# Columns of tiles 16 to 31 from a second layout of x, and a first block whose carry, counts and store come one to two steps later

## The chip, the cores and the metric

The kernel runs on one core of a Trainium2 chip. What is timed is the device time of one execution in microseconds (us). Three executions of the kernel before took 832.69, 831.65 and 831.66 us; the median is 831.66 us.

## The reference: what is computed

x is 4096 rows of 512. A first part normalizes each row (layer norm, then an RMS norm), projects it with a 512 x 512 matrix, and adds a row of a context table, chosen by running sums over a mask. That table is a linear recurrence over 3202 context rows. A second part is a layer norm and a feed-forward network of hidden size 2048. Cut to what matters:

```python
x = x + xattn(_layernorm(x), ctx_2048, mask, W_in, b_in, g_res, g_init)
#   h = rmsnorm(embeds, g_res) @ W_in.T + b_in
#   s[t] = a * s[t-1] + dt * bcoef * (rmsnorm(ctx, g_init)[t, :512] / dt)
#   plug = clip(cumsum(boundary_mask) - 1, 0, plen - 1)
#   xattn = s[plug] + h
x = x + gelu(_layernorm(x) @ w1 + b1) @ w2 + b2
```

## The kernel before, in words

**Two stages.** The first stage takes x in 32 tiles of 128 rows (steps t = 0 to 31 of a Python loop that is written out on every engine). The second takes 8 groups of 512 rows through the two feed-forward products. All products are in split precision: a float32 operand is written as a high part plus a low part, and three matmuls (high by high, low by high, high by low) stand for one. L889 to L891 are these three.

**One tile of the first stage.** TensorE needs the tile with its columns on the partitions. In the kernel before, tiles 0 to 19 are loaded in rows and transposed by TensorE (`transpose_first`, L872, four 128x128 transposes into a PSUM bank). Tiles 20 to 31 (`HOSTED`) come a second time, from an array `x_cols` in which x is already laid out by columns; SyncE loads them into free quarters of `w_raw` (L445), and `columns(t)` (L195) says where they are. ScalarE rounds the columns to the high part (`tile_high`, L717), VectorE subtracts to get the low part (`tile_low`, L1070), TensorE makes the twelve 512-wide matmuls of `project(t)` (L893), and VectorE scales the result and adds x (`tile_add`, L1078). Each engine keeps its own order: at step t VectorE first does `tile_add(t-1)`, then `tile_low(t+2)`, then whatever else the loop puts at that step, then the statistics of a later tile (L1065, L1066). `project(t)` waits for `tile_low(t)` and, through its PSUM bank, for `tile_add(t-3)`.

**The context blocks beside the tiles.** The recurrence runs over blocks of 512 rows, four rows per partition. Two blocks (`cl`, then `cl_next`) are made in the first stage. For each, VectorE does three scans within a partition (`scan_row`, L1084: both inputs in SBUF), TensorE multiplies the last row by `band` to get what comes over from other partitions (`carry`, L921, into the PSUM tile `acc[3]`), VectorE adds it to the four rows (`add_carry`, L1102, one input in PSUM), and SyncE stores the block to `scan_table` (`store_block`, L387). Both blocks use the same `acc[3]`, so the second `carry` waits on the semaphore `block_ready` until VectorE has read the first. GpSimd (POOL) waits for both stores before it gathers rows from the table (L577).

**The counts.** `count_positions` (L932, TensorE) sums one-hot products; `count_rows` (L1181 to L1184, VectorE) makes running counts of them; `count_before` (L938 and L939, TensorE, at step 20, waiting on `cnt_ready`) sums these over partitions; `finish_plug` (VectorE, step 20) makes the indices of the gather.

**GpSimd in these steps.** `scales` (L539, L540) makes the factors of four tiles once their statistics are there, and `add_bias` (L572) adds a bias to a 128x512 tile, both operands in SBUF; steps 15 to 17 have three of these, behind the `scales` of step 15, which waits for the statistics of tile 19.

Of the kernel before, what the change touches and what calls it, by code (L numbers as in the profile page):

```python
# [36 lines left out]
NT = S // P  # L37
K = D // P
# [20 lines left out]
LAG = 2  # L59
STORE0 = 16  # L60
WARM = 14
# [11 lines left out]
def wait_apart(engine, sem, value):  # L73

    engine.wait_ge(sem, value)
    engine.nop(nofuse=True)
# [32 lines left out]

HOSTED = tuple(range(20, NT))  # L110


def xattn_ffn(nc, x, x_cols, ctx, mask, w_in, b_in, g_res, g_init, w1, b1, w2, b2, out):
# [11 lines left out]
    with es:  # L125
# [69 lines left out]
        def columns(t):  # L195

            if t not in HOSTED:
                return first_bank[t % 3][:]
            u = t - HOSTED[0]
            q = 1 + u // K  # L200
            return w_raw[:, u % K, q * D:(q + 1) * D]
# [150 lines left out]
        def _(sp):  # L352
# [80 lines left out]
            for t in range(NT):  # L433
                if t > TI:
                    store_x1(t - 1)
                while loaded < min(NT, t + (11 if t < 12 else 13)):
# [5 lines left out]
                    loaded += 1  # L442
                if 5 <= t < 5 + len(HOSTED) // 2:
                    for u in (2 * (t - 5), 2 * (t - 5) + 1):
                        sp.dma_start(columns(HOSTED[u]), x_cols[HOSTED[u], :, :]).then_inc(cols_loaded[u], 16)  # L445
                if t == STORE0:
                    store_block(0, cl)
                if t == STORE0 + 2:
                    store_block(1, cl_next)
# [6 lines left out]
                if t == 29:  # L456
                    wait_apart(sp, x_lo, HOSTED[K])
                    load_w1(1)
                    load_w2(1)
            load_high_half(NA, 2)  # L460
            load_high_half(NA, 3)
            store_x1(NT - 1)
            wait_apart(sp, x_lo, HOSTED[2 * K])
            load_w1(2)
# [404 lines left out]
        def _(pe):  # L869
# [99 lines left out]
            for t in range(3, NT):  # L969
                if t + 2 < HOSTED[0]:  # L970
                    transpose_first(t + 2)
                if t == 4:
                    mask_totals()
                if t == 15:
                    pe.wait_ge(consts_made, 5)
                    carry(0, cl, acc[3][:])
                if t == 16:
                    count_positions()
# [70 lines left out]
        def _(dve):  # L1049
# [184 lines left out]
            for t in range(NT):  # L1234
# [25 lines left out]
                if t == 15:  # L1260
                    add_carry(0, acc[3][:], cl, (0, 1))
                    scan_row(1, cl_next, 1)
                if t == 16:
                    add_carry(0, acc[3][:], cl, (2, 3))
                    scan_row(1, cl_next, 2)
                    scan_row(1, cl_next, 3)
                if t == 17:
                    count_rows()
                if t == 18:
                    add_carry(1, acc[3][:], cl_next, (0, 1))  # L1270
                    add_carry(1, acc[3][:], cl_next, (2, 3))
                if t == 20:
                    finish_plug()
# [108 lines left out]
```

## Time and profile before

| what | value |
|---|---|
| median of three executions | 831.66 us |
| the profiled execution's own time | 834.93 us |
| its span, first to last instruction | 833.2 us |
| granted TensorE clock over the span | 1.000 of full speed |
| busy: PE / DVE / ACT / POOL | 822.3 / 315.9 / 294.0 / 258.0 us |
| first stage (steps 0 to 31) | up to about 118 us of the span |

All stretches below are read from the profiled execution, 1.7 us of whose time lies outside the span. "PE" is TensorE's matmuls, "PEld" its weight loads, "DVE" VectorE, "ACT" ScalarE, "POOL" GpSimd, "SPq" SyncE's DMA queue. Matmuls are pipelined, so one of 512 columns is shown with 0.39 us although the next starts 0.23 us after it; the distance from start to start is the pace. A VectorE instruction's successor likewise starts some 0.08 us before the shown end.

### The profile page before, as it was taken

The page shows a single profiled execution, that of the slowest core. Times are in us where ns is not written, and L with a number is a line of the kernel's source. Part 1 is how long each engine was busy: PE and PEld are TensorE (multiplying, and loading weights), DVE is VectorE, ACT ScalarE, POOL GpSimd, SP SyncE. Part 2 cuts the span into 40 slices and gives each one's busy share as a digit, 9 for nine tenths or more (in the row PEclk, how much of TensorE's full clock was granted, in tenths as well). Part 3 has the DMA queues.
Part 4 walks back from the last instruction along what each step waited for, and adds up shares of the span by engine and source line. Part 5 has one row for each costly group of instructions (what it writes and reads, how often), then busy time and mean ns, then how long its engine had stood idle before and what let it go on. Part 6 is the DMA issues. An engine that isn't in the chain of part 4 may idle for free.

```text
span 833.2 us, 10703 instructions
## 1 busy us (share of the span) xinstructions
PE 822.3 (99%) x3722; PEld 675.9 (81%) x3722; DVE 315.9 (38%) x513; ACT 294.0 (35%) x542; POOL 258.0 (31%) x238
## 2 busy tenths in 40 slices
PE   7999999999999999999999999999999999999998
PEld 5877878788888888888888888888888888888886
DVE  5899852665141423233332423143113411241112
ACT  5668446422622253224422262222222222222221
POOL 2254659940633035301630062305300250011000
PEclk9999999999999999999999999999999999999999
DMA  9988994260236022602233113302300240010001
GB/s 227 281 263 282 291 301 153 89 163 22 68 102 160 0 76 88 167 7 74 72 113 80 50 58 103 50 0 101 51 1 1 79 72 0 0 50 1 1 0 51
DMA packets 39057, 78.11 MB, mean 94 GB/s; under 512 B 6369, under 2 KB 6369, under 8 KB 37265
## 3 DMA queue, kind: packets, MB, share of 16 engines
q1 hardware_dynamic: 30052, 65.95, 24.3%
q0 software_dynamic: 4608, 8.39, 6.4%
q10 hardware_dynamic: 4368, 3.42, 1.5%
q8 instruction: 14, 0.23, 0.1%
q14 instruction: 15, 0.11, 0.1%
HBM read 51.02 MB, written 22.84 MB: 89 GB/s over the span
## 4 chain that ended last, share of the span: by engine, by line
PE 81%; POOL 7%; DVE 4%; DMA 3%; issue 2%; SPq 1%; ACT 1%; ACTq 0%; POOLq 0%; DVEq 0%
PE acc L889 13%; PE acc L890 13%; PE acc L891 13%; PE h_bank L889 13%; PE h_bank L890 13%; PE h_bank L891 13%; DMA xa_odd<-in_x_dram 2%; POOL w_lo L545 2%; PE t_bank L948 2%; POOL x_cur L651 1%; POOL x_next L577 1%; DMA scan_table<-cl_next 1%; POOL cl L564 1%; POOL w_lo L551 1%; DVE h_lo L1070 1%
## 5 line engine op out<-in xcount | busy, mean ns | idle before, releaser
L1303 DVE TENSOR_TENSOR h_lo<-g_f,h_hi 128x512 fp32r<-128x512 f32 x128 | 101.1, 790 | 432.1 <-ACT g_f L826 432.1
L824 ACT ACTIVATE h_hi<-h_bank,b_c 128x512 fp32r<-128x512 f32 x128 | 87.9, 687 | 429.5 <-PE h_bank L891 425.9
L889 PE MATMUL h_bank<-xt_hi,w_hi 128*128 128x512 f32 x512 | 199.9, 390 | 0.6 <-POOL w_lo L545 0.6
L889 PE MATMUL acc<-w_hi,h_hi 128*128 128x512 f32 x512 | 199.8, 390 | 0.0
L891 PE MATMUL h_bank<-xt_hi,w_lo 128*128 128x512 f32 x512 | 199.3, 389 | 0.0
L890 PE MATMUL h_bank<-xt_lo,w_hi 128*128 128x512 f32 x512 | 199.2, 389 | 0.0
L891 PE MATMUL acc<-w_hi,h_lo 128*128 128x512 f32 x512 | 199.2, 389 | 0.0
L890 PE MATMUL acc<-w_lo,h_hi 128*128 128x512 f32 x512 | 199.2, 389 | 0.0
L889 PEld LDWEIGHTS h_bank<-xt_hi,w_hi 128*128 128x128 f32 x512 | 96.1, 188 | 20.7 <-issue 1.0
L891 PEld LDWEIGHTS h_bank<-xt_hi,w_lo 128*128 128x128 f32 x512 | 96.1, 188 | 20.0
L891 PEld LDWEIGHTS acc<-w_hi,h_lo 128*128 128x128 f32 x512 | 96.1, 188 | 20.0
L890 PEld LDWEIGHTS h_bank<-xt_lo,w_hi 128*128 128x128 f32 x512 | 96.1, 188 | 19.7
L889 PEld LDWEIGHTS acc<-w_hi,h_hi 128*128 128x128 f32 x512 | 96.1, 188 | 19.7
L890 PEld LDWEIGHTS acc<-w_lo,h_hi 128*128 128x128 f32 x512 | 96.1, 188 | 19.7
L826 ACT ACTIVATE g_f<-h_bank,b_c 128x512 f32<-128x512 f32 x128 | 87.2, 681 | 0.4 <-DVE h_lo L1303 0.4
L577 POOL DMA_INDIRECT x_next<-scan_table,idx x32 | 51.7, 1617 | 72.6 <-DMA scan_table<-cl 59.6
L564 POOL TENSOR_TENSOR cl<-cl,g_init_b 128x512 f32<-128x512 f32 x24 | 31.9, 1335 | 99.1 <-ACT ch L735 93.1
L651 POOL TENSOR_TENSOR x_cur<-x_next,b_b 128x512 f32<-128x512 f32 x32 | 44.4, 1419 | 56.9 <-DMA out_dram<-x_cur 56.6
L572 POOL TENSOR_TENSOR x_next<-x_next,b_in_b 128x512 f32<-128x512 f32 x32 | 45.6, 1424 | 32.0 <-DMA x_next<-x_part 28.4
L588 POOL TENSOR_SCALAR va_b<-mv_b 128x4 f32<-128x4 f32 x7 | 1.4, 197 | 171.8 <-DVE mv_b L1201 171.8
L889 PE MATMUL acc<-win_hi,h_hi 128*128 128x512 f32 x88 | 36.2, 411 | 2.9 <-DVE win_lo L1175 1.9
L747 ACT ACTIVATE xt_hi<-t_bank 128x512 fp32r<-128x512 f32 x32 | 17.4, 597 | 50.7 <-PE h_bank L891 37.4
(168 smaller groups left out, 701.1 us busy)
## 6 DMA issues: line engine op xcount, KB each, us to landing
out_dram<-x_cur SPq DMA_DIRECT2D x32, 256.0 KB, 2.1
x_next<-x_part SPq DMA_DIRECT2D x7, 1024.0 KB, 5.0
w_raw<-in_L_ffn_w_dram SPq DMA_DIRECT2D x6, 1024.0 KB, 9.0
scan_table<-cl SPq DMA_DIRECT2D x6, 896.0 KB
ch<-in_ctx_dram SPq DMA_DIRECT2D x20, 256.0 KB, 2.9
cl<-in_ctx_dram SPq DMA_DIRECT2D x5, 1024.0 KB
xa_odd<-in_x_dram SPq DMA_DIRECT2D x16, 256.0 KB, 7.3
x_part<-xa_odd SPq DMA_DIRECT2D x16, 256.0 KB, 3.9
```

The lines of the kernel that those rows point to most:

```text
L545: pool.tensor_tensor(w_lo[:, k, r], w_raw[:, k, r], w_hi[:, k, r].bitcast(F32), ALU.subtract).then_inc(w1_ready, 1)
L564: pool.tensor_tensor(rows[:, j, :], rows[:, j, :], g_init_b[:], ALU.mult).then_inc(g_scaled, 1)
L572: step(pool.tensor_tensor(x_next[:, i, :], x_next[:, i, :], b_in_b[:], ALU.add))
L577: pool.indirect_dma_start(x_next[:, i, :], None, rows, bass.IndirectOffsetOnAxis(ap=idx[:, i:i + 1].bitcast(U32), axis=0), compute_op=ALU. ...
L651: ins = pool.tensor_tensor(x_cur[:, i, :], x_next[:, i, :], b2_b[:], ALU.add)
L747: act.activation(xt_hi[:, :, i * P:(i + 1) * P], t_bank[i % 2][:].rearrange("p (k r) -> p k r", k=K), ACT.Copy).then_inc(t_hi, 1)
L824: act.activation(h_hi[:, m % HB, :], h_bank[m % 2][:], ACT.Gelu, bias=b1_c[:, m:m + 1])
L826: act.activation(g_f32[:], h_bank[m % 2][:], ACT.Gelu, bias=b1_c[:, m:m + 1]).then_inc(gelu_done, 1)
L889: nc.tensor.matmul(dst, a_hi, b_hi, start=first, stop=False)
L890: nc.tensor.matmul(dst, a_hi, b_lo, start=False, stop=False)
L891: return nc.tensor.matmul(dst, a_lo, b_hi, start=False, stop=final)
L1303: dve.tensor_tensor(h_lo[:, m % HB, :], g_f32[:], h_hi[:, m % HB, :].bitcast(F32), ALU.subtract).then_inc(h_split, 1)
```

## The change

Tiles 16 to 19 join those that come from `x_cols`. There are places for 12 such tiles in `w_raw`, so tiles 28 to 31 take the places of 16 to 19 and are loaded at SyncE's steps 21 and 22 instead of 9 and 10. For the first context block, TensorE's `carry` goes from step 15 to 16, VectorE's `add_carry` from steps 15 and 16 to 16 and 17, now behind the second block's scans, and its store from step 16 to 17. The positions are counted at step 17 instead of 16, and VectorE's `count_rows` goes from step 17 to the end of step 18, behind the second block's `add_carry`. `store_block(1)` stays at step 18.

```diff
@@ -57,7 +57,7 @@
 WC = 2048
 HB = 4
 LAG = 2
-STORE0 = 16
+STORE0 = 17
 WARM = 14
 LEAD = 4
 
@@ -107,7 +107,8 @@
     return sum(1 for v in tiles if v < t)
 
 
-HOSTED = tuple(range(20, NT))
+HOSTED = tuple(range(16, NT))
+PLACES = 12
 
 
 def xattn_ffn(nc, x, x_cols, ctx, mask, w_in, b_in, g_res, g_init, w1, b1, w2, b2, out):
@@ -197,7 +198,7 @@
             if t not in HOSTED:
                 return first_bank[t % 3][:]
             u = t - HOSTED[0]
-            q = 1 + u // K
+            q = (3, 1, 2, 3)[u // K]
             return w_raw[:, u % K, q * D:(q + 1) * D]
 
         def x1(t):
@@ -440,12 +441,14 @@
                         wait_x1(loaded - XR)
                     load_tile(loaded)
                     loaded += 1
-                if 5 <= t < 5 + len(HOSTED) // 2:
-                    for u in (2 * (t - 5), 2 * (t - 5) + 1):
+                if 5 <= t < 5 + PLACES // 2 or t in (21, 22):
+                    for u in (2 * (t - 5), 2 * (t - 5) + 1) if t < 21 else (2 * (t - 15), 2 * (t - 15) + 1):
+                        if u >= PLACES:
+                            wait_apart(sp, x_lo, HOSTED[u - PLACES] + 1)
                         sp.dma_start(columns(HOSTED[u]), x_cols[HOSTED[u], :, :]).then_inc(cols_loaded[u], 16)
                 if t == STORE0:
                     store_block(0, cl)
-                if t == STORE0 + 2:
+                if t == STORE0 + 1:
                     store_block(1, cl_next)
                 if t == 22:
                     load_high_half(NA, 0)
@@ -454,13 +457,13 @@
                     wait_apart(sp, table_stored, STORED + BLOCK_STORED * 2)
                     load_low_half(NA)
                 if t == 29:
-                    wait_apart(sp, x_lo, HOSTED[K])
+                    wait_apart(sp, x_lo, HOSTED[2 * K])
                     load_w1(1)
                     load_w2(1)
             load_high_half(NA, 2)
             load_high_half(NA, 3)
             store_x1(NT - 1)
-            wait_apart(sp, x_lo, HOSTED[2 * K])
+            wait_apart(sp, x_lo, HOSTED[3 * K])
             load_w1(2)
             load_w2(2)
             wait_apart(sp, x_lo, NT)
@@ -971,10 +974,10 @@
                     transpose_first(t + 2)
                 if t == 4:
                     mask_totals()
-                if t == 15:
+                if t == 16:
                     pe.wait_ge(consts_made, 5)
                     carry(0, cl, acc[3][:])
-                if t == 16:
+                if t == 17:
                     count_positions()
                 if t == 19:
                     pe.wait_ge(block_ready, 1)
@@ -1258,17 +1261,17 @@
                 if t == 14:
                     one_hots_p(MJ // 2, MJ)
                 if t == 15:
-                    add_carry(0, acc[3][:], cl, (0, 1))
                     scan_row(1, cl_next, 1)
                 if t == 16:
-                    add_carry(0, acc[3][:], cl, (2, 3))
                     scan_row(1, cl_next, 2)
                     scan_row(1, cl_next, 3)
+                    add_carry(0, acc[3][:], cl, (0, 1))
                 if t == 17:
-                    count_rows()
+                    add_carry(0, acc[3][:], cl, (2, 3))
                 if t == 18:
                     add_carry(1, acc[3][:], cl_next, (0, 1))
                     add_carry(1, acc[3][:], cl_next, (2, 3))
+                    count_rows()
                 if t == 20:
                     finish_plug()
                 for v in (t + LEAD,) if t < 22 else (2 * t - 18, 2 * t - 17) if t < 25 else ():
```

On VectorE, steps 15 to 17. Before (L1102 adds the carry, L1084 scans, L1065 and L1066 are the statistics of tile 19, L1078 `tile_add`, L1070 `tile_low`, L1181 and L1183 the counts):

```order
L1102 SCALAR_TENSOR_TENSOR cl<-acc,cl 128x512 x2
L1084 SCALAR_TENSOR_TENSOR cl_next<-cl_next 128x512
L1065 BN_STATS st_a<-xa_even 128x6
L1066 BN_AGGR mv_a<-st_a 128x2
L1078 SCALAR_TENSOR_TENSOR xa_odd<-acc,ra,xa_odd 128x512
L1070 TENSOR_TENSOR h_lo<-t_bank,h_hi 128x512
L1102 SCALAR_TENSOR_TENSOR cl<-acc,cl 128x512 x2
L1084 SCALAR_TENSOR_TENSOR cl_next<-cl_next 128x512 x2
L1078 SCALAR_TENSOR_TENSOR xa_even<-acc,ra,xa_even 128x512
L1070 TENSOR_TENSOR h_lo<-t_bank,h_hi 128x512
L1181 TENSOR_SCALAR cnt<-h_bank 128x32
L1183 TENSOR_TENSOR cnt<-cnt 128x8 x3
```

The same place in the changed kernel, whose lines are three further down (L1105 adds the carry, L1087 scans, L1081 `tile_add`, L1073 `tile_low`):

```order
L1087 SCALAR_TENSOR_TENSOR cl_next<-cl_next 128x512
L1068 BN_STATS st_a<-xa_even 128x6
L1069 BN_AGGR mv_a<-st_a 128x2
L1081 SCALAR_TENSOR_TENSOR xa_odd<-acc,ra,xa_odd 128x512
L1073 TENSOR_TENSOR h_lo<-w_raw,h_hi 128x512
L1087 SCALAR_TENSOR_TENSOR cl_next<-cl_next 128x512 x2
L1105 SCALAR_TENSOR_TENSOR cl<-acc,cl 128x512 x2
L1081 SCALAR_TENSOR_TENSOR xa_even<-acc,ra,xa_even 128x512
L1073 TENSOR_TENSOR h_lo<-w_raw,h_hi 128x512
L1105 SCALAR_TENSOR_TENSOR cl<-acc,cl 128x512 x2
```

The first pair of carries moved behind the statistics and the scans, the second pair behind `tile_low(19)`; the counts are gone from here, and the low parts read `w_raw` in SBUF where they read a PSUM bank.

VectorE's step 18, before:

```order
L1078 SCALAR_TENSOR_TENSOR xa_even<-h_bank,ra,xa_even 128x512
L1070 TENSOR_TENSOR h_lo<-w_raw,h_hi 128x512
L1102 SCALAR_TENSOR_TENSOR cl_next<-acc,cl_next 128x512 x4
L1078 SCALAR_TENSOR_TENSOR xa_even<-acc,ra,xa_even 128x512
L1070 TENSOR_TENSOR h_lo<-w_raw,h_hi 128x512
```

and in the changed kernel, where L1184 to L1187 are `count_rows`:

```order
L1081 SCALAR_TENSOR_TENSOR xa_even<-h_bank,ra,xa_even 128x512
L1073 TENSOR_TENSOR h_lo<-w_raw,h_hi 128x512
L1105 SCALAR_TENSOR_TENSOR cl_next<-acc,cl_next 128x512 x4
L1184 TENSOR_SCALAR cnt<-h_bank 128x32
L1186 TENSOR_TENSOR cnt<-cnt 128x8 x3
L1187 COPY row_tot<-cnt 128x8
L1081 SCALAR_TENSOR_TENSOR xa_even<-acc,ra,xa_even 128x512
```

The counts now stand between the second block's carries and `tile_add(18)`, as the last work of step 18.

## Rows read from the trace of the kernel before

**Rows 1.** Waits of PE over the whole span: total, times, longest.

```profile
PE t_bank L948 <- DVE n_rows L1212: 0.6, 1, 0.6
PE h_bank L889 <- POOL w_lo L545: 0.6, 1, 0.6
```

**Rows 2.** Timeline of PE, steps 15 to 28: start us, length us, instruction.

```profile
63.78 0.60 PE L877 MATMUL acc<-ident,xa_even 128*128 128x128 f32 x4
...
67.86 0.60 PE L877 MATMUL t_bank<-ident,xa_even 128*128 128x128 f32 x4
...
72.06 0.60 PE L877 MATMUL t_bank<-ident,xa_even 128*128 128x128 f32 x4
...
75.27 0.39 PE L889 MATMUL acc<-win_hi,h_hi 128*128 128x512 f32 x1
...
78.14 1.10 PE L921 MATMUL acc<-cl_next,band 128*128 128x512 f32 x2
...
82.16 0.29 PE L938 MATMUL h_bank<-row_tot,tri 128*128 128x8 f32 x2
...
82.53 0.47 PE L889 MATMUL h_bank<-win_hi,h_hi 128*128 128x512 f32 x1
...
104.44 0.39 PE L889 MATMUL acc<-win_hi,h_hi 128*128 128x512 f32 x1
...
107.16 0.39 PE L889 MATMUL h_bank<-win_hi,h_hi 128*128 128x512 f32 x1
```

**Rows 3.** Timeline of DVE, from step 15 to the start of step 19.

```profile
70.00 1.28 DVE L1102 SCALAR_TENSOR_TENSOR cl<-acc,cl 128x512 f32<-128x512 f32 x2
71.19 0.68 DVE L1084 SCALAR_TENSOR_TENSOR cl_next<-cl_next 128x512 f32<-128x512 f32 x1
71.91 0.69 DVE L1065 BATCH_NORM_STATS2 st_a<-xa_even 128x6 f32<-128x512 f32 x1
...
72.82 0.75 DVE L1078 SCALAR_TENSOR_TENSOR xa_odd<-acc,ra,xa_odd 128x512 f32<-128x512 f32 x1
...
75.28 2.71 DVE L1084 SCALAR_TENSOR_TENSOR cl_next<-cl_next 128x512 f32<-128x512 f32 x2
77.91 0.74 DVE L1078 SCALAR_TENSOR_TENSOR xa_even<-acc,ra,xa_even 128x512 f32<-128x512 f32 x1
78.57 0.67 DVE L1070 TENSOR_TENSOR h_lo<-t_bank,h_hi 128x512 fp32r<-128x512 f32 x1
79.17 0.17 DVE L1181 TENSOR_SCALAR cnt<-h_bank 128x32 f32<-128x32 f32 x1
...
80.11 0.75 DVE L1078 SCALAR_TENSOR_TENSOR xa_even<-h_bank,ra,xa_even 128x512 f32<-128x512 f32 x1
...
81.38 2.48 DVE L1102 SCALAR_TENSOR_TENSOR cl_next<-acc,cl_next 128x512 f32<-128x512 f32 x4
83.77 0.74 DVE L1078 SCALAR_TENSOR_TENSOR xa_even<-acc,ra,xa_even 128x512 f32<-128x512 f32 x1
```

**Rows 4.** Timeline of POOL: the three biases.

```profile
74.44 4.69 POOL L572 TENSOR_TENSOR x_next<-x_next,b_in_b 128x512 f32<-128x512 f32 x3
```

**Rows 5.** Lines L1084 and L1070, all instances: duration ns min/median/max.

```profile
L1084 DVE SCALAR_TENSOR_TENSOR cl_next<-cl_next x3: 680/1008/1669, 71.2 to 76.3; 128x512 f32<-128x512 f32 x3
L1070 DVE TENSOR_TENSOR h_lo<-w_raw,h_hi x12: 679/681/1036, 80.8 to 108.0; 128x512 fp32r<-128x512 f32 x12
```

**Rows 6.** Timeline of PE, then of POOL: the end of the first stage.

```profile
109.98 1.11 PE L948 MATMUL t_bank<-ident,n_rows 128*128 128x128 f32 x8
...
114.50 1.11 PE L948 MATMUL t_bank<-ident,n_rows 128*128 128x128 f32 x8 [0.65 <-DVE n_rows L1212]
...
108.21 1.05 POOL L584 TENSOR_TENSOR rb<-va_b,neg_half 128x2 f32<-128x2 f32 x1
```

**Rows 7.** Timeline of POOL: the first gather, behind the second block's store.

```profile
91.79 2.28 POOL L577 DMA_INDIRECT x_next<-scan_table,idx  x1 [4.04 <-DMA scan_table<-cl_next]
```

**Rows 8.** DMA in a stretch: window, length, granted clock, DMA share, GB/s.

```profile
80.00:85.00 5.00, 1.00 1.03 413
```

## The prediction

> **What bounds the kernel now.** I read the waits of TensorE first. Over 833 us they come to two entries of 0.6 us beside the start-up [rows 1], so TensorE's own stream sets the end, and whatever moves that stream moves the time one for one. Next I read TensorE's timeline through steps 15 to 20 [rows 2], because the transposes go there, and then VectorE's over the same stretch [rows 3]. VectorE has no idle entry from 70.00 to 83.77: it is as full as TensorE there, and the change puts two results that TensorE waits for later in VectorE's order. That is where the case is decided. Last come the end of the first stage [rows 6], where a wait can give time back, and the store that releases the gathers [rows 7].
>
> **What the transposes are worth.** A tile with its transposes takes 75.27 - 72.06 = 3.21 us, one without 107.16 - 104.44 = 2.72 us [rows 2]. Four tiles lose 0.49 each: 1.96 us. The carry costs TensorE (67.86 - 63.78) - 3.21 = 0.87 us; it only changes its step. In the kernel before, `project(18)` ends at 75.27 + 2.72 = 77.99, so in the changed kernel TensorE reaches step 19 at about 76.0. If nothing else bound it, the gain would be about 2.0 us.
>
> **What VectorE now makes of it.** VectorE enters step 15 at 70.00 in both kernels: up to there it and ScalarE are full, or wait for each other and for GpSimd, not for transposes. Prices from start to start [rows 3]: two carries 71.19 - 70.00 = 1.19; a scan 71.91 - 71.19 = 0.72; statistics 72.82 - 71.91 = 0.91; `tile_add` 78.57 - 77.91 = 0.66; `tile_low` 79.17 - 78.57 = 0.60; counts 80.11 - 79.17 = 0.94; four carries 83.77 - 81.38 = 2.39. The new order:
> scan 70.72, statistics 71.63, `tile_add(15)` 72.29, `tile_low(18)` 72.89. GpSimd's three biases start 74.44 - 72.82 = 1.62 after the statistics [rows 3, 4], so now at 73.25.
> Two scans: alone 1.3 (680 ns is the shortest [rows 5]), but beside the biases they took 77.91 - 75.28 = 2.63 in the kernel before. Now the first runs before the first bias, and the second waits for that bias: I take 2.3, to 75.2. Two carries 76.4, `tile_add(16)` 77.05. `tile_low(19)` now has both inputs in SBUF, and the third bias runs until about 77.7: 1.1 instead of 0.60, to 78.15. Two carries: `block_ready` at 79.35.
> So TensorE, ready at 76.0, waits some 3.4 us for the first block's carries before it can begin the second `carry`. With 0.87 + 2.72 it ends `project(19)` at 83.0.
> VectorE goes on: `tile_add(17)`, `tile_low(20)` to 80.6; the second block's carries need TensorE's product, 1.10 long [rows 2], about 0.1 of wait, to 83.1; the counts to 84.05. `count_before` waits for them at the head of step 20, a second wait of 1.0. Before, it was ready for TensorE: 80.11 against 82.16. From 84.05 to `project(20)` I count 0.75: 0.37 for the two small products [rows 2] and an estimate of 0.38 for waking and the first weight load. `project(20)` starts at 84.8, before at 82.53: **2.3 us later**.
>
> The check on this is short. The changed kernel gives VectorE the same list of work between 70.00 and the end of step 18, so it ends near 83.77 as before; only now TensorE cannot start `project(20)` until it has. The sum of the contention is the unknown. Bounds: none at all would end step 18 at 83.77 - 1.3 = 82.45 (+0.7 us for TensorE); every two-SBUF instruction there (three, after the first scan) waiting out a whole bias of 1.3 would end it at 86.3 (+4.5). I take +2.3, nearest to the row of 2.63 for two scans.
>
> What the trace shows of this contention is that L1084 took 680 ns with GpSimd silent and 1669 ns among the biases, and a low part read from `w_raw` went from 681 to 1036 ns once [rows 5], while the PSUM-fed carries and `tile_add` kept their length. The Trainium skill, "SBUF — State Buffer", section "SBUF: two separate sides", gives a rule for it: a VectorE instruction with two SBUF inputs and a GpSimd instruction that reads SBUF hold one port pair in turn, whole instructions long. The trace agrees, by 1008 and 1669 against 680 ns. The rule speaks against this change: moving the columns of tiles 16 to 19 from PSUM to SBUF makes `tile_low(19)` such an instruction. Without the rule the sum at `project(20)` would be about 0.5 less.
>
> **What is given back.** From step 20 on VectorE has room again, and TensorE runs unbroken to step 30. There, before, its sequence stood idle 0.65 us until the second half of the second norm was there at 114.50; with the 0.1 to 0.2 lost in starting again I call it 0.8, and 0.1 more at the first half [rows 6]. That norm goes back to GpSimd's factors at 108.21, after gathers that wait for the second store, and they do not move with TensorE. With TensorE 2.3 later the factors are there in time. The path from TensorE's own transposes over ScalarE and VectorE back to it fits too: it took 114.50 - 109.98 = 4.5 us [rows 6], and part of that were statistics on VectorE that will now be done by then. I count 0.9 of 2.3 as given back. The other wait, 0.6 us for GpSimd's `w_lo` in the first group [rows 1], starts from the first feed-forward result, moves with TensorE and gives nothing.
>
> **The DMAs.** As many column tiles as before are loaded at SyncE's steps 5 to 10. The four late ones (1 MB) stand behind `tile_add(20)` and `tile_add(21)`, which now follow `project(20)` at 84.8 + 2.72 and one tile later: issued near 88.5 and 91. ScalarE needs the first after `project(24)`, at 84.8 + 5 x 2.72 = 98.4: free. The first block's store comes at 79.4, after its carries, instead of 75.3 (where the scans of [rows 3] follow them), into a stretch that is full (share 1.03 at 413 GB/s [rows 8]); 0.9 MB at 413 GB/s is 2.3 us. The second store could be issued once the carries ended at 81.38 + 2.48 = 83.9 [rows 3], and the first gather started at 91.79, having waited 4.04 for it [rows 7]; issued 0.7 sooner with up to 2.3 in front, it may land 1.6 later. Against TensorE's delay of 2.3 that costs at most 0.2, which I leave to the range. If the later columns were to slow the gathers too, it would be the last rival below.
>
> **Sum.** +2.3 - 0.9 = +1.4 us on the profiled execution: 834.93 + 1.4 = 836.3. The median stands 3.3 below that execution, so 831.66 + 1.4 = **833.1 us**.
>
> **Rivals.**
> A, the gain arrives: VectorE gets through its work sooner than I think, `block_ready` comes by 76 and the counts by 79, and TensorE keeps 2.0: 829.7 us. For it: TensorE is 99% busy and the work leaves it. Against: it needs 3 us that VectorE doesn't have.
> B, little contention: VectorE ends step 18 near 82.5, TensorE is 0.7 late and all of that is given back: 831.7 us. Against: the biases follow the statistics at the same distance and meet three such instructions.
> C, the clock: the granted clock is 1.00 in all rows I read, but no TensorE wait there is as long as the 3.4 us expected now. If the clock fell to its 1.2 GHz level, one tile at half the rate costs 2.72 more: 835.8 us. The Trainium skill, "TensorE: Matmul & The Clock Gate", states that the array falls to 1.2 GHz after idling; no run here shows it yet.
> D, slower by the gathers: the crowded stores and the late columns hold up the gathers. It decides once GpSimd's factors of 108.21 slip by more than 2.3 + 0.8 us; a slip of 4.5, twice the 2.3 of one store's transfer, costs 1.4 more: 834.5 us.
>
> **Chances.** Forecast 0.67, A 0.10, B 0.09, C 0.06, D 0.08. 0.2% (1.66 us) is about what a measurement of this kernel can tell from no change, and +1.4 stands just inside: of the forecast's 0.67 I give 0.36 to under 1.66 and 0.31 above. So faster 0.10; within 0.2% 0.36 + 0.09 = 0.45; slower 0.31 + 0.14 = 0.45. The range: the lower bound of the contention with all given back is 831.7, and some way to A 831.0; above, the bound of +4.5 less 0.9 would be 835.3, and D is inside: 831.0 to 835.4. A and C are left out.
>
> **What would show it.** Right: TensorE waits about 3.4 us before the second `carry` on VectorE, about 1 us before `count_before`; two of the instructions with two SBUF inputs are lengthened; `project(20)` starts near 84.8 and the wait at the second norm is gone. Wrong: `block_ready` by 77, or no wait before `count_before`; a granted clock under 1.00 speaks for C; a longer wait at the second norm for D.

## The result, and the profile after

The changed kernel is slower. Its median is 835.93 us (834.00 to 836.91, 9 executions) beside 831.65 us for the kernel before on the same chip; the ratio is 1.0044, 95% interval 1.0034 to 1.0054, or 3.7 us. (Ratios are estimated over all executions of a set, so they are not exactly those of the medians.) A second set of executions on another occasion gave 834.60 beside 831.82 us, ratio 1.0029 (1.0020 to 1.0039), or 2.4 us. The forecast was +1.4 us. Single executions of one kernel lie up to 5 us apart, so every ratio below carries its interval.

The waits of TensorE over the whole span (without the start-up; the one on w_lo stood in the kernel before as well, [rows 1]):

```profile
PE acc L924 <- DVE cl L1105: 2.6, 1, 2.6
PE h_bank L892 <- POOL w_lo L548: 0.6, 1, 0.6
PE h_bank L941 <- DVE row_tot L1187: 0.2, 1, 0.2
```

Two of the three are new, and they are the two that were forecast: before the second `carry` on the first block's carries (L1105), and before `count_before` on the counts (L1187). The timeline of TensorE at that place:

```profile
74.41 0.39 PE L892 MATMUL acc<-win_hi,h_hi 128*128 128x512 f32 x1
...
77.87 2.07 PE L924 MATMUL acc<-cl_next,band 128*128 128x512 f32 x2 [2.62 <-DVE cl L1105]
78.95 1.41 PE L892 MATMUL acc<-win_hi,h_hi 128*128 128x512 f32 x1
...
83.45 0.39 PE L941 MATMUL h_bank<-row_tot,tri 128*128 128x8 f32 x2 [0.24 <-DVE row_tot L1187]
83.92 0.48 PE L892 MATMUL h_bank<-win_hi,h_hi 128*128 128x512 f32 x1
```

The `carry` behind the wait takes 2.07 us, where it took 1.10 before [rows 2], and the first matmul of `project(19)` shows 1.41 us instead of 0.39. The windows of the same kernel show that the granted clock fell with it (length, busy time of PE, PEld, DVE, ACT, POOL, granted clock, DMA share, GB/s). These are means over 5 us. Read us by us, the clock is 1.00 up to 77, 0.72 from 77 to 78, 0.50 from 78 to 80, which is its lower level of 1.2 GHz, 0.58 from 80 to 81, and 1.00 again from 81.

```profile
75.00:80.00 5.00, 2.38 (x5) 1.10 (x4) 4.09 (x7) 4.87 (x14) 4.38 (x4) 0.74 0.91 296
80.00:85.00 5.00, 4.76 (x21) 3.60 (x21) 4.86 (x12) 2.91 (x10) 0.00 (x0) 0.92 1.02 341
```

VectorE, the same stretch, answering to [rows 3]:

```profile
69.20 0.69 DVE L1087 SCALAR_TENSOR_TENSOR cl_next<-cl_next 128x512 f32<-128x512 f32 x1
...
72.08 1.41 DVE L1087 SCALAR_TENSOR_TENSOR cl_next<-cl_next 128x512 f32<-128x512 f32 x2
73.41 1.28 DVE L1105 SCALAR_TENSOR_TENSOR cl<-acc,cl 128x512 f32<-128x512 f32 x2
...
75.27 1.35 DVE L1073 TENSOR_TENSOR h_lo<-w_raw,h_hi 128x512 fp32r<-128x512 f32 x1
76.54 1.28 DVE L1105 SCALAR_TENSOR_TENSOR cl<-acc,cl 128x512 f32<-128x512 f32 x2
...
79.98 2.48 DVE L1105 SCALAR_TENSOR_TENSOR cl_next<-acc,cl_next 128x512 f32<-128x512 f32 x4 [0.91 <-PE acc L924]
...
83.22 0.17 DVE L1187 COPY row_tot<-cnt 128x8 f32<-128x8 f32 x1
```

VectorE enters step 15 at 69.20. The two scans took their short time in this execution (1.41, against 2.71 in [rows 3]), the low part of tile 19 took twice its time (1.35), and VectorE then stood 0.91 us for the slow `carry`.

At the end of the stage the second norm's transposes follow one another with no wait between them, 3.87 us apart, where [rows 6] had 4.52 with a wait of 0.65:

```profile
111.25 1.03 PE L951 MATMUL t_bank<-ident,n_rows 128*128 128x128 f32 x8
115.12 1.11 PE L951 MATMUL t_bank<-ident,n_rows 128*128 128x128 f32 x8
118.82 0.39 PE L892 MATMUL h_bank<-xt_hi,w_hi 128*128 128x512 f32 x1
```

**A measure that doesn't scatter.** What moves single executions is mostly ahead of step 15: VectorE enters it anywhere between 67.23 and 70.00. From the first feed-forward matmul (118.82 here, 118.20 in the first profile of before) to the end of the span, all but one of the profiled executions take 714.9 to 715.1 us (715.4 in that one). So I call the distance from VectorE's entry into step 15 to the first feed-forward matmul the **stretch**, and compare kernels by it and by the ratio. "To 20" is the distance from the same entry to the start of `project(20)`, where it still is the work right behind the counts.

| kernel | entry | to 20 | stretch | against 47.47 | ratio of times (interval) |
|---|---|---|---|---|---|
| before, first profile | 70.00 | 12.53 | 48.20 | +0.73 | |
| before, profiled again | 67.67 | 12.53 | 47.47 | 0 | 1.0000 (0.9992 to 1.0009) |
| changed, first | 69.20 | 14.72 | 49.62 | +2.15 | 1.0044 (1.0034 to 1.0054) |
| changed, again | 67.49 | 15.33 | 50.24 | +2.77 | 1.0029 (1.0020 to 1.0039) |
| columns alone | 67.54 | 13.01 | 47.91 | +0.44 | 0.9995 (0.9983 to 1.0007) |
| order alone | 67.34 | 14.08 | 48.99 | +1.52 | 1.0015 (1.0003 to 1.0028) |
| two banks | 68.86 | 14.14 | 51.75 | +4.28 | 1.0018 (1.0000 to 1.0036) |
| filler, first | 68.83 | 13.85 | 48.76 | +1.29 | 1.0007 (0.9993 to 1.0020) |
| filler, again | 67.23 | 13.80 | 48.72 | +1.25 | 1.0023 (1.0014 to 1.0032) |
| no waits | 67.29 | | 48.01 | +0.54 | 1.0008 (0.9999 to 1.0017) |
| changed, biases late | 67.47 | 14.06 | 48.96 | +1.49 | 1.0025 (1.0015 to 1.0035) |
| counts at 20 | 69.03 | | 47.03 | -0.44 | 1.0002 (0.9994 to 1.0011) |
| counts at 20, rb earlier | 67.55 | | 48.18 | +0.71 | 1.0010 (1.0001 to 1.0019) |
| columns, biases late | 69.58 | | 48.44 | +0.97 | 1.0009 (1.0000 to 1.0018) |

0.001 is 0.83 us. Each ratio is taken against executions of the kernel before on the same occasion. On that of the first four experiments (columns alone, order alone, two banks, filler first) the kernel before was itself slower and more scattered, 833.51 us in the median and 831.47 to 835.84 in 31 executions, against 831.82 and 831.94 on the two later ones; so the ratios of those four are to be compared with the others' with care. The reference 47.47 is the second profile of the kernel before; why not the first is the main finding below.

### The profile page after: what moved, and what is told of

Same layout as the page of the kernel before. It is cut to its first block, busy times and chain, and to the rows that moved or that the text cites. A ratio compares the mean times of both kernels' runs of the same rounds, so it can differ in the third digit from the quotient of the medians.

```text
span 833.9 us, 10675 instructions
## 1 busy us (share of the span) xinstructions
PE 821.1 (98%) x3706; PEld 674.7 (81%) x3706; DVE 319.6 (38%) x513; ACT 294.2 (35%) x542; POOL 258.4 (31%) x238
## 4 chain that ended last, share of the span: by engine, by line
PE 84%; DVE 5%; POOL 4%; DMA 2%; issue 2%; SPq 1%; ACT 1%; ACTq 0%; DVEq 0%; POOLq 0%
PE acc L892 14%; PE acc L894 14%; PE acc L893 14%; PE h_bank L892 13%; PE h_bank L894 13%; PE h_bank L893 13%; DMA xa_odd<-in_x_dram 2%; PE t_bank L951 2%; POOL w_lo L548 1%; DVE h_lo L1073 1%; POOL x_cur L654 1%; POOL cl L567 1%; POOL w_lo L554 1%; DVE st_a L1068 1%; SPq L363 0%
## 5 line engine op out<-in xcount | busy, mean ns | idle before, releaser
L1306 DVE TENSOR_TENSOR h_lo<-g_f,h_hi 128x512 fp32r<-128x512 f32 x128 | 103.8, 811 | 428.1 <-ACT g_f L829 428.1
```

What stands on the lines that cost most here:

```text
L1306: dve.tensor_tensor(h_lo[:, m % HB, :], g_f32[:], h_hi[:, m % HB, :].bitcast(F32), ALU.subtract).then_inc(h_split, 1)
```

## The experiments

In the diffs, lines with - and + are against the kernel named.

**Columns alone** (label e1_cols_only): the changed kernel's columns of tiles 16 to 31 in the order of work of the kernel before.

```diff
-HOSTED = tuple(range(20, NT))
+HOSTED = tuple(range(16, NT))
+PLACES = 12
...
```

> Only the columns of tiles 16 to 19 come from the second layout; the order of carries, counts and stores is that of the kernel before. Theory 1 (TensorE now waits for two results that VectorE gives late, the first block's carries and the counts): these are early again, so TensorE reaches step 19 some 2 us sooner but finds only tile_low(19) late, on a VectorE that is full to about 79.8 us. No wait over 2 us in one piece, granted clock 1.000, time within 0.5 us of the kernel before (831.2 to 832.1). Theory 2 (what is above my 1.4 us comes from the TensorE clock after the long wait): the same here, since the long wait is gone. Theory 3 (late loads of the columns of tiles 28 to 31 and crowded DMAs slow the end of the stage): the loads are as late as in the changed kernel, so it stays 2 us or more slower than before.

The ratio is 0.9995 (0.9983 to 1.0007): no change that can be measured. Where the 1.96 us of transposes went is written in TensorE's timeline (each row that waited between steps 13 and 18):

```profile
61.66 1.10 PE L924 MATMUL acc<-cl,band 128*128 128x512 f32 x2 [0.35 <-DVE cl L1087]
66.04 0.82 PE L935 MATMUL h_bank<-oh_q,oh_p 128*128 128x32 bf16 x26 [0.52 <-DVE oh_p L1161]
75.69 1.10 PE L924 MATMUL acc<-cl_next,band 128*128 128x512 f32 x2 [0.57 <-DVE cl_next L1087]
77.28 0.50 PE L892 MATMUL acc<-win_hi,h_hi 128*128 128x512 f32 x1 [0.49 <-DVE h_lo L1073]
```

0.35 + 0.52 + 0.57 + 0.49 = 1.93 us, all on VectorE: the work that left TensorE came back as waits, nearly one for one. So in this profile VectorE sets the pace here, and the transposes had filled time in which TensorE would have waited for it.

The columns are not quite free either. `project(20)` starts 0.48 us later after VectorE's entry than before, and `tile_low(19)`, which now reads `w_raw` in SBUF, takes 1.10 us where it took 0.67 from a PSUM bank [rows 3]:

```profile
76.13 1.10 DVE L1073 TENSOR_TENSOR h_lo<-w_raw,h_hi 128x512 fp32r<-128x512 f32 x1
```

**Order alone** (e2_order_only): before's columns, the changed order.

```diff
-STORE0 = 16
+STORE0 = 17
...
```

> Only the order changes; tiles 16 to 19 are transposed by TensorE as before and all columns are loaded early. Theory 1: VectorE ends step 18 at the same time as in the changed kernel less about 0.5 us of contention at tile_low(19), which reads PSUM again; TensorE arrives 2 us later and so waits about 1 us for the first block's carries and about 1 us for the counts. Project(20) starts some 1.8 us later than before, 0.9 is given back: +0.9 us (832.6). Theory 2: the wait is too short for the clock to fall, so nothing comes on top and the granted clock is 1.000. Theory 3: no late columns, so no more than before.

It is 1.0015 (1.0003 to 1.0028), 1.2 us slower, with the two new waits in small:

```profile
76.32 1.12 PE L921 MATMUL acc<-cl_next,band 128*128 128x512 f32 x2 [0.74 <-DVE cl L1102]
80.95 0.39 PE L938 MATMUL h_bank<-row_tot,tri 128*128 128x8 f32 x2 [0.76 <-DVE row_tot L1184]
```

So most of the loss comes with the order: +1.52 in the stretch. With the columns added, TensorE arrives 2 us sooner and waits longer for the same VectorE: 2.62 + 0.24 and 3.34 us in the two profiles of the changed kernel, against 0.74 + 0.76 here.

**Two banks** (e3_two_banks): the second block's `carry` goes into another bank and no longer waits for the first block's.

```diff
-                    pe.wait_ge(block_ready, 1)
-                    carry(1, cl_next, acc[3][:])
+                    carry(1, cl_next, acc[2][:])
...
-                    add_carry(1, acc[3][:], cl_next, (0, 1))
+                    add_carry(1, acc[2][:], cl_next, (0, 1))
```

> The changed kernel, but the second carry goes to the PSUM tile acc[2] and does not wait for the first block's carries. Theory 1: the wait of 3 us before it goes, the one before count_before stays and becomes the long one (TensorE ends project(19) near 79, counts near 82.4): project(20) starts about 0.9 sooner than in the changed kernel, because VectorE no longer waits for TensorE's product: +0.5 to +0.9 us against the kernel before when the clock holds. Theory 2: a wait of about 3 us still stands there, so the granted clock still falls in some executions and costs 1.7 to 3.3 us there. Theory 3: as slow as the changed kernel, +3.7.

The first wait went and the second grew to take its place:

```profile
PE h_bank L941 <- DVE row_tot L1186: 2.8, 1, 2.8
```

The ratio is 1.0018 (1.0000 to 1.0036), not to be told from the changed kernel's 1.0029 (1.0020 to 1.0039), though with a wider spread: 832.97 to 838.29 us. The profiled execution (837.79) is one of the long ones, and its windows show why this one is long:

```profile
80.00:85.00 5.00, 2.88 (x9) 2.49 (x10) 4.79 (x14) 3.11 (x9) 1.20 (x2) 0.69 0.93 299
85.00:90.00 5.00, 5.00 (x16) 3.91 (x15) 1.98 (x6) 0.63 (x1) 0.19 (x1) 0.63 0.95 324
```

Behind a wait of 2.75 us the whole of `project(20)` ran at the lower level of 1.2 GHz (granted clock 0.50 from 82 to 88), 83.00 to 88.27, 5.27 instead of 2.72 us, with no wait left to hide it. The stretch is 4.28 us longer than before's.

**Filler matmuls** (e4_filler, and the same kernel once more as f2_filler): twelve 512-column matmuls into a bank nobody reads, at the place of the wait. They change no output.

```diff
+                    for k in range(12):
+                        nc.tensor.matmul(acc[2][:], win_hi[:, k % K, 0:P], win_hi[:, k % K, :], start=True, stop=True)
                     pe.wait_ge(block_ready, 1)
```

> The changed kernel with twelve matmuls of 512 columns (0.23 us each, 2.7 in all) added on TensorE in front of its wait for the first block's carries, into the PSUM tile acc[2]; nothing reads their result. They fill most of a wait that the profile shows with 3.0 us. Theory 2 (the clock falls because TensorE stands idle): granted clock 1.000 in all executions and the time falls from +3.7 to +1.4 us or a little more against the kernel before (833 to 833.5). Theory 1 alone, with no part of the clock: no change, +3.7. Theory 3: no change, +3.7.

> The changed kernel with the twelve filler matmuls of 2.7 us in front of the wait for the first block's carries, now on the same chip as the changed kernel. Theory 2: 0.5 to 1.5 us faster than the changed kernel, granted clock 1.00 between 75 and 90 us, the wait before the counts 0.7 us as it was, project(20) about 13.9 us after VectorE's entry into step 15 (changed kernel 14.7). Theory 1 without a clock: the same time as the changed kernel, since the filler ends before the result it stands in front of.

The ratios are 1.0007 (0.9993 to 1.0020) and 1.0023 (1.0014 to 1.0032). TensorE's timeline in the first:

```profile
74.96 2.88 PE L984 MATMUL acc<-win_hi 128*128 128x512 f32 x12
77.69 1.02 PE L924 MATMUL acc<-cl_next,band 128*128 128x512 f32 x2
```

and the window of 75 to 80 of the second:

```profile
75.00:80.00 5.00, 4.80 (x20) 3.21 (x18) 4.93 (x11) 4.35 (x13) 2.58 (x3) 1.00 1.00 369
```

In both profiles the granted clock stays at 1.00 here, the `carry` is back at 1.02, and the stretch is 48.76 and 48.72. The first profile of the changed kernel (49.62) is the fair partner: there too the scans took 1.41 us and `tile_low(19)` 1.35 (here 1.37), so the 0.86 us between them are the clock's. In the second (50.24) the scans also took 0.97 us more. The wait itself stays, filled instead of idle, so +1.25 remains. By the times the filler's gain is not shown: beside f2's 1.0023 the changed kernel had 1.0029 on the same chip, and the intervals overlap.

**The changed kernel again** (a1_changed), as it is.

> The changed kernel once more, beside the others of this comparison, since executions of the kernel before spread from 831.5 to 835.8 us with the DMAs of the first 40 us. Counted from VectorE's entry into step 15 to the end of the span, the profiles give 763.2 us before and 764.7 changed. Theory 1 (two late results, +1.5 in that count) and the clock (theory 2, up to 1.7 or 3.3 more in executions where it falls) give +1.5 to +3.5 us against the kernel before; a rest count above 764.7 only where the granted clock is under 1.00 between 75 and 90 us.

1.0029 (1.0020 to 1.0039). The same two engines, another execution:

```profile
70.42 2.38 DVE L1087 SCALAR_TENSOR_TENSOR cl_next<-cl_next 128x512 f32<-128x512 f32 x2
...
74.58 1.33 DVE L1073 TENSOR_TENSOR h_lo<-w_raw,h_hi 128x512 fp32r<-128x512 f32 x1
...
81.57 0.17 DVE L1187 COPY row_tot<-cnt 128x8 f32<-128x8 f32 x1
```

```profile
77.16 1.13 PE L924 MATMUL acc<-cl_next,band 128*128 128x512 f32 x2 [3.34 <-DVE cl L1105]
77.72 0.79 PE L892 MATMUL acc<-win_hi,h_hi 128*128 128x512 f32 x1
...
82.46 0.28 PE L941 MATMUL h_bank<-row_tot,tri 128*128 128x8 f32 x2
```

Here the scans are lengthened as forecast (2.38; 2.3 was put) and the wait is 3.34 us (3.4 was put). The clock fell again (0.85 and 0.81 in the windows of 75 to 80 and 80 to 85), so `project(19)` ran from 77.72 to 82.46, 4.74 instead of 2.72 us. At full clock it would have ended at 80.44 and waited for the counts of 81.74; so the clock cost about 0.7 us (an estimate), and the rest of the slow tile lay inside that wait.

**No waits** (e5_no_waits): two banks, and `count_before` and `finish_plug` at step 22 in place of 20.

```diff
-                if t == 20:
+                if t == 22:
                     count_before()
```

> The changed kernel with both waits gone: the second carry goes to acc[2] and waits for nothing of the first block, and TensorE's count_before and VectorE's finish_plug stand at step 22 instead of 20. Theory 1: project(20) starts about 10.3 us after VectorE's entry into step 15 (12.5 before, 14.7 changed), 2.2 us sooner than before, and what the transposes are worth arrives; the second norm at the end of the stage then takes back 0.8 to 1.4 of it, since GpSimd's gathers start only about 1.5 us sooner. Rest count 761.5 to 762.5: 1 to 1.5 us faster than the kernel before, no fall of the clock. Theory 3 (DMAs, late columns) or a rival by which the columns themselves cost: as slow as the changed kernel.

It missed: 1.0008 (0.9999 to 1.0017) where I put 1 to 1.5 us faster than before. Neither old wait is left, but TensorE has new ones, again on VectorE, the longest 1.31 us. (A further one of 0.67 us is on n_rows, at the end of the stage.)

```profile
PE acc L892 <- DVE h_lo L1072: 1.8, 3, 1.3
```

The low part of a tile now stands behind the second block's carries and the counts in VectorE's order. Freed of the long waits the kernel is as fast as before, not faster. That the length of VectorE's list holds the stretch is my reading of it; "counts at step 20", below, tests it.

**Biases late** (e6_bias_late): the changed kernel with GpSimd's biases 1 to 3 at its step 20 in place of 15 to 17.

```diff
-                if 14 <= t <= 17:
-                    pool.wait_ge(acc_read, t - 13)
-                    add_bias(t - 14)
+                for i in (0,) if t == 14 else (1, 2, 3) if t == 20 else ():
+                    pool.wait_ge(acc_read, i + 1)
+                    add_bias(i)
```

> The changed kernel with three of GpSimd's biases behind the factors of step 19 instead of between those of steps 15 and 19. If GpSimd's biases lengthen tile_low(19), which reads two inputs in SBUF (1.35 us for 0.68 in the changed kernel), it takes 0.68 now, the first block's carries come 0.67 sooner, TensorE's wait is about 2.3 instead of 3.0 and project(20) starts 0.4 to 0.7 sooner, less if tile_low(20) is lengthened in its place; the clock falls less often. +0.5 to +1.5 us against the kernel before. If the lengthening comes from something else (ScalarE's write of the same high part, a DMA into w_raw), tile_low(19) keeps its 1.35 us and the time is that of the changed kernel.

1.0025 (1.0015 to 1.0035), not to be told from the changed kernel's 1.0029. VectorE's rows show that the edit did what it should at its place, and that the cost moved:

```profile
70.40 1.41 DVE L1087 SCALAR_TENSOR_TENSOR cl_next<-cl_next 128x512 f32<-128x512 f32 x2
...
73.58 0.68 DVE L1073 TENSOR_TENSOR h_lo<-w_raw,h_hi 128x512 fp32r<-128x512 f32 x1
...
76.03 1.65 DVE L1073 TENSOR_TENSOR h_lo<-w_raw,h_hi 128x512 fp32r<-128x512 f32 x1
```

Scans and `tile_low(19)` are at their short times, TensorE's wait fell to 1.80 us (the granted clock fell here too, to 0.66 in the window of 75 to 80), and `tile_low(20)`, now beside the moved biases (74.44 to 78.82), takes 1.65 instead of 0.68.

**Columns, biases late** (e8_cols_bias_late): the same edit on the columns alone.

> The columns part of the change alone (order of work as in the kernel before), and GpSimd's biases 1 to 3 moved from its steps 15 to 17 to step 20. If the biases lengthen VectorE's scans, the two scans of cl_next that took 2.69 us take 1.4, TensorE's wait of 0.57 us for cl_next before the second carry and that of 0.49 us for h_lo go, and it is 0.8 to 1.1 us faster than with the columns alone: 831.2 to 831.6. If the length of the scans has another cause, they stay near 2.7 and the ratio is that of the columns alone, 1.000.

The scans went from 2.69 to 1.40 as expected, but it is not faster: 1.0009 (1.0000 to 1.0018).

```profile
74.90 1.40 DVE L1087 SCALAR_TENSOR_TENSOR cl_next<-cl_next 128x512 f32<-128x512 f32 x2
...
77.70 2.48 DVE L1186 TENSOR_TENSOR cnt<-cnt 128x8 f32<-128x8 f32 x3
...
80.97 1.14 DVE L1073 TENSOR_TENSOR h_lo<-w_raw,h_hi 128x512 fp32r<-128x512 f32 x1
```

Three additions of 128x8 elements, 0.60 us together in the kernel before, take 2.48 beside the biases (77.14 to 81.56). So the two runs show that the biases lengthen VectorE's instructions with two SBUF inputs, and that a bias takes its toll from whichever such instruction stands beside it, even one of 128x8 elements (174 to 1189 ns, against 174 to 184 in the kernel before).

**The kernel before again** (b1_before_again), as it is.

> The kernel before, word for word, profiled once more. In its first profile the two scans of cl_next took 2.71 us beside GpSimd's biases, and from VectorE's entry into step 15 to the end of the span were 833.2 - 70.00 = 763.2 us. Yet the lowest time of each kernel with an edit stands about 0.9 us further over the lowest of the kernel before than the differences of this stretch say. If that first profile was one of its worse executions in this stretch, this one shows a stretch of 762.2 to 762.8, with the two scans at 1.4 to 2.0 us; if the 0.9 us lie ahead of step 15, it shows 763.2 again and an entry near 66.4 us. Ratio 1.000 either way.

The ratio is 1.0000, and the stretch 47.47, 0.73 shorter than in the first profile. The difference is not where I had looked: "to 20" is 12.53 in both, and the two scans take 2.72 here and 2.71 there. It lies at the end of the stage. Here is GpSimd (the row of rb answers to the one in [rows 6], the gather to [rows 7]), then VectorE's first n_rows, then TensorE:

```profile
89.02 1.81 POOL L577 DMA_INDIRECT x_next<-scan_table,idx  x1 [3.59 <-DMA scan_table<-cl_next]
...
104.41 0.69 POOL L584 TENSOR_TENSOR rb<-va_b,neg_half 128x2 f32<-128x2 f32 x1
```

```profile
106.31 1.00 DVE L1212 TENSOR_SCALAR n_rows<-x_next,mv_b,rb 128x512 f32<-128x512 f32 x2
...
107.57 1.03 PE L948 MATMUL t_bank<-ident,n_rows 128*128 128x128 f32 x8
...
111.44 1.11 PE L948 MATMUL t_bank<-ident,n_rows 128*128 128x128 f32 x8
```

From VectorE's entry, rb ends at 105.10 - 67.67 = 37.43, in the first profile at 109.26 - 70.00 = 39.26, and TensorE is ready for its transposes at 39.90 and 39.98. So in this execution the wait of 0.65 us for the second norm doesn't exist. In the first profile VectorE had stood waiting for rb:

```profile
109.38 1.00 DVE L1212 TENSOR_SCALAR n_rows<-x_next,mv_b,rb 128x512 f32<-128x512 f32 x2 [0.66 <-POOL rb L584]
```

All fourteen profiles fit one account. The second n_rows starts 4.52 to 4.54 us after the first (between them VectorE has its own full list), and TensorE's second transposes 0.6 us behind it. TensorE's own work from the first transposes to the second is 3.87 us. Where the first n_rows starts 1.25 us or more ahead of TensorE's first transposes there is no wait (ten profiles); where it starts only 0.6 ahead, TensorE waits 0.65 to 0.67 (four). What made rb late in the first profile is less sure: the first gather started 21.79 after the entry there and 21.35 here and took 2.28 instead of 1.81 us, and small differences followed up to rb.

**Counts at step 20** (e7_counts_at_20): "no waits" with VectorE's `count_rows` at step 20 in place of 18.

```diff
+                if t == 20:
                     count_rows()
```

> The kernel with the second carry in a bank of its own and count_before at step 22, and VectorE's count_rows moved from its step 18 to its step 20, behind the subtraction for which TensorE waited 1.31 us. If VectorE's order at that place is all that holds the stage, the 1.31 us shrink to about 0.3 and the kernel is 1.0 us faster than its parent (831.6 beside a kernel before at 831.8). If GpSimd's chain at the end of the stage (last gather, ra, four subtractions w_lo, rb, which gave a wait of 0.67 us for n_rows in the parent) is the floor, TensorE's wait for n_rows grows from 0.67 to about 1.6 us and the time is the parent's, 832.6.

1.0002 (0.9994 to 1.0011). The wait of 1.31 us fell to 0.36 (row below), as VectorE's order would have it; another, behind the second `carry`, was 0.58 instead of 0.30; and the wait for n_rows stayed at 0.66 and didn't grow:

```profile
82.61 0.50 PE L892 MATMUL acc<-win_hi,h_hi 128*128 128x512 f32 x1 [0.36 <-DVE h_lo L1072]
```

The first n_rows waited 0.66 us for rb in this run and in "no waits", and "no waits" was no long execution (832.14 beside a median of 832.62), so this wait is not only an accident of long ones. The stretch is 0.98 shorter than that of "no waits"; by the times (1.0008 and 1.0002) that is not shown. It is as fast as the kernel before and no faster.

**rb earlier** (e9_counts_and_rb): on top of it, rb of the first two tiles ahead of the last two of the four w_lo.

```diff
-            for k in range(K):
-                low_w1(0, k, 1)
+            low_w1(0, 0, 1)
+            low_w1(0, 1, 1)
             first_scale(slice(0, 2), rb_first)
+            low_w1(0, 2, 1)
+            low_w1(0, 3, 1)
```

> The same as the kernel with count_rows at step 20, and on GpSimd rb of the first two tiles of the second norm goes ahead of the last two of the four subtractions w_lo (which take 6.0 us together), so that it comes about 3 us earlier. If GpSimd's chain is the floor, the wait for n_rows goes to 0 and this is 1.5 us faster than the kernel with count_rows at step 20 alone, about 831.0. If the end of the stage is held by TensorE's own work or by the statistics on VectorE, it is the same as that kernel.

A miss: 1.0010 (1.0001 to 1.0019). rb moved to its place, yet the wait stayed:

```profile
103.25 0.69 POOL L587 TENSOR_TENSOR rb<-va_b,neg_half 128x2 f32<-128x2 f32 x1
103.92 2.54 POOL L548 TENSOR_TENSOR w_lo<-w_raw,w_hi 128x512 fp32r<-128x512 f32 x2
```

```profile
105.40 1.60 DVE L1074 TENSOR_TENSOR h_lo<-w_raw,h_hi 128x512 fp32r<-128x512 f32 x1
106.92 0.99 DVE L1216 TENSOR_SCALAR n_rows<-x_next,mv_b,rb 128x512 f32<-128x512 f32 x2
```

```profile
107.51 1.11 PE L953 MATMUL t_bank<-ident,n_rows 128*128 128x128 f32 x8
112.04 1.11 PE L953 MATMUL t_bank<-ident,n_rows 128*128 128x128 f32 x8 [0.65 <-DVE n_rows L1216]
```

The rows above name the reason. n_rows no longer waits for rb, but the `tile_low` just ahead of it takes 1.60 instead of 0.68 us, beside the two w_lo that the edit moved there (103.92 to 106.46). So the first n_rows starts 0.59 us ahead of the transposes again, and the second follows 4.53 later. The edit took one delay away and made another of the same size: it is the contention of the biases once more, with another pair of instructions.

## Why the prediction was partly right

The direction and the main mechanism held; the size did not, and one term was wrong in kind. The median of 835.93 lies 2.8 above the forecast and 0.5 beyond the range's upper end; by the ratio, 831.66 x 1.0044 = 835.3, it lies just inside. The second set's 834.60 lies inside.

- **What VectorE makes of it: right.** TensorE waits for the first block's carries, 2.62 and 3.34 us (3.4 forecast), then for the counts, 0.24 us and none (1.0 forecast; the slow tile in between used it up). `project(20)` starts 14.72 and 15.33 after VectorE's entry; the forecast was 14.8, from 12.53. Order alone (+1.52 in the stretch) and columns alone (+0.44, no gain in the times) show that the order makes most of the loss and that the columns give nothing. From VectorE's next instruction behind the counts (83.31) to `project(20)` (83.92) it took 0.61 us, where I had put 0.75.
- **The contention: right in kind, variable in size.** In one profile two instructions are lengthened (2.38 and 1.33), in the other only `tile_low(19)` (1.35). The Trainium skill, "SBUF — State Buffer", section "SBUF: two separate sides", has it that a VectorE instruction with two SBUF inputs and a GpSimd instruction that reads SBUF lock each other out for whole instructions. The 128x8 additions at up to 1189 ns against a median of 176 agree; it would be hard to explain by a shared bandwidth that so short an instruction takes so long.
- **The clock, rival C: its condition came true, its price did not.** It fell in both profiles of the changed kernel. I had given this 6%, and the price of a whole slow tile, 2.72 us. What it cost is about 0.9 us in the first (the `carry` of 2.07 held up VectorE by 0.91; filler matmuls take that away) and 0.7 in the second. That the first profile's `project(20)` came out at 14.72, so near the forecast of 14.8, is luck: `block_ready` came 0.8 us earlier than forecast (less contention), and VectorE then stood 0.91 us for the slow `carry` where I had put 0.1. Only where no second wait followed, in "two banks", did it cost the full 2.55. By the times alone the clock's share is not shown. In the changed kernel's second set, the three executions with a mean clock of 1.000 took 833.00 to 833.76 us, the six at 0.997 or 0.998 took 833.79 to 835.06, and the two at 0.996 took 835.71 and 835.86, which would fit; but the eight executions of "filler, again" at 1.000 took 832.69 to 835.87 us.
- **What is given back: this step failed.** I put 0.9 us on the room before the second norm's transposes, 0.8 of it for the wait of 0.65 [rows 6]. Against that one profile the term was right: "to 20" grew by 2.19 and the stretch by 1.42, so 0.77 was given back. But the profiled execution was 3.3 us over the median of its kernel, and the second profile of the kernel before has no such wait. Against it the changed kernel loses 2.19 at `project(20)` and 2.15 at the feed-forward, and the second time 2.80 and 2.77: nothing comes back. Columns alone (0.48 and 0.44), order alone (1.55 and 1.52), both fillers (1.32 and 1.29, 1.27 and 1.25) and biases late (1.53 and 1.49) say the same: whatever is lost at `project(20)` arrives whole. I took the long execution's time down to the median as a shift, and kept a wait that was part of what made it long.
- **The DMAs: right.** The first gather starts at 90.00 after a wait of 2.70 us for the store, 20.80 after VectorE's entry (21.79 and 21.35 in the two profiles of the kernel before), so it did not land later, as I had thought it might; rival D is out. The second store is 896 and 96 KB, which is 2.5 us at 413 GB/s, and not the 0.9 MB and 2.3 us that I wrote; the sum doesn't use it. Rival A is out with its 3 us that VectorE doesn't have, and B as well.

So +2.15 to +2.77 in the stretch answers for the 2.4 us of the second set. The 3.7 us of the first set are 1 to 1.5 more, and its one profile shows no further place for them. A candidate is the clock: both profiles of the changed kernel have a mean clock of 0.998, but four of the nine executions of the first set had 0.996 (835.93 to 836.91 us), against two of eleven in the second. None of those was profiled. In "two banks" and "filler, first" the clock also fell once at the start-up, from 13 to 17 us, so a mean of 0.996 can come from two falls in one execution. That remainder stays open.

## What to carry to other kernels

Where two engines are both full, ask which one waits for which before taking work from one of them: here TensorE's 1.96 us of transposes filled time in which it would have waited for VectorE, and removing them gave 1.93 us of waits. Moving a result later in the order of the fuller engine costs the other engine the shift less the time by which the result had been early: the counts came 4.0 us later, had been ready 2.0 us before TensorE needed them, and `project(20)` started 2.2 us later. And before a wait is counted as room in which a delay can disappear, see whether it is there in another profile too; one profile, 3 us over the median, is not enough. (Two don't say how often the wait occurs, either.)

## What was not expected of the hardware

- The granted clock went to 0.50, the lower level of 1.2 GHz, with TensorE's waits of 2.62, 3.34 and 2.75 us, and with the wait of 1.80 us in "biases late". In the changed kernel's first profile it fell at 77.4, before the end of the wait (77.87), in the second at 78.5, 1.3 us behind its end (77.16). With the waits of 1.31 us in "no waits" and 0.74 in order alone it stayed at 1.00, and twelve filler matmuls kept it at 1.00.
- What GpSimd's biases cost a VectorE instruction doesn't go by its size. 128x8 additions took up to 1189 ns, and moving the biases only chose another victim; so did moving w_lo.
- GpSimd suffers too. In the changed kernel's first profile its power on 128x4 elements took 1.58 us beside VectorE's scans of 72.08:

```profile
71.46 1.58 POOL L543 TENSOR_TENSOR ra<-va_a,neg_half 128x4 f32<-128x4 f32 x1
```

It takes 1.02 in the second, where the scans were the ones to wait.
